# Four groups of PE signals moved from the last product to a drain, in two phases of a graph network kernel

## What is computed

```
x = layernorm(x + L0(x, edge_attr_64, src, dst, edge_type_32))   # relation attention
x = layernorm(x + L1(x, edge_index, 4))                          # four propagation steps
x = layernorm(x + L2(x, edge_index, edge_attr_128))              # gated convolution
x = layernorm(x + L3(x, edge_index))                             # two attention layers

# L0, its first part
h_proj = einsum('nd,rde->rne', h, relation_weight)
t_r = h_proj[etype, src]; h_r = h_proj[etype, dst]
# L2
z = concatenate([x[dst], x[src], edge_attr])
msg = sigmoid(z @ W_f + b_f) * softplus(z @ W_s + b_s)
out = relu(x + segment_sum(msg, dst))
```

## Time and profile before

| | us |
|---|---|
| median of 3 runs (7758.99 to 7787.47) | 7766.42 |
| span of the profiled execution | 7865.6 |
| PE busy in it | 4297.8 (55%) |
| DVE busy | 4772.7 (61%) |
| GpSimd busy | 3733.3 (47%) |
| ACT busy | 2362.7 (30%) |

### The profile page before, as it was taken

How to read it: one execution, slowest core, us unless ns; L and a number is a source line. 1 busy time by engine, 2 the same in 40 slices (tenths; PEclk the granted TensorE clock), 3 DMA queues, 4 the chain that set the end, 5 groups by cost and what they waited for, 6 DMA issues and landing times. The chain is left out here.

```text
span 7865.6 us, 104440 instructions
## 1 busy us (share of the span) xinstructions
PE 4297.8 (55%) x26852; PEld 3458.2 (44%) x26923; DVE 4772.7 (61%) x7334; ACT 2362.7 (30%) x3661; POOL 3733.3 (47%) x4217
## 2 busy tenths in 40 slices
PE   5777777310279545555535444444695444444397
PEld 2677776310179545555523222222683222222396
DVE  4666666688521156566547666666665766666675
ACT  5444444117322145555522111111222111111121
POOL 3666566100200166666625555553654555655363
PEclk9555555555589777777767666666896766666696
DMA  8677777895578533233225656564654666656462
GB/s 313 191 219 212 222 203 226 228 236 191 215 250 307 183 112 115 96 117 114 91 72 147 159 152 156 154 157 119 135 134 114 157 158 155 160 150 158 100 140 75
DMA packets 1472089, 1296.30 MB, mean 165 GB/s; under 512 B 1257993, under 2 KB 1297567, under 8 KB 1459038
## 3 DMA queue, kind: packets, MB, share of 16 engines
q1 hardware_dynamic: 902378, 671.59, 28.5%
q0 software_dynamic: 167008, 441.69, 21.0%
q10 hardware_dynamic: 402580, 181.62, 8.4%
HBM read 942.23 MB, written 351.27 MB: 164 GB/s over the span
## 5 line engine op out<-in xcount | busy, mean ns | idle before, releaser
L2503 POOL DMA_INDIRECT rows_p<-node_rows,stage_i x1632 | 1546.5, 948 | 1228.0 <-issue 978.9
L2557 PE MATMUL psZ<-parts_r,hot_t 128*128 x4896 | 1164.3, 402 | 1360.5 <-DVE lz L2638 867.7
L2557 PEld LDWEIGHTS psZ<-parts_r,hot_t 128*128 128x128 bf16 x4896 | 590.0, 121 | 1938.6 <-issue 1624.4
L2646 DVE TENSOR_TENSOR psZ<-psZ,rows_p 128x1320 f32<-128x1320 f32 x408 | 626.5, 1536 | 768.9 <-remote 283.0
L731 POOL DMA_INDIRECT rows_s<-hpx,hpST x784 | 741.4, 946 | 486.4 <-issue 203.8
L1961 POOL DMA_INDIRECT both<-table,srcI x784 | 741.9, 946 | 431.5 <-issue 211.1
L749 PE MATMUL psP<-window,pair_hot 128*128 x3136 | 701.9, 416 | 249.0 <-ACT pair_hot L771 146.6
L749 PEld LDWEIGHTS psP<-window,pair_hot 128*128 128x128 f32 x3136 | 672.8, 325 | 279.2 <-issue 279.0
L828 DVE SCALAR_TENSOR_TENSOR pair_run<-pair_run,same_c,psP 128x64 f32<-128x64 f32 x1568 | 440.2, 281 | 469.1 <-PE psP L749 209.1
L2953 PE MATMUL ps_steps<-A,xs 128*65 128x125 f32 x5184 | 578.8, 272 | 137.8 <-DVE A L2971 93.1
L2638 DVE SCALAR_TENSOR_TENSOR lz<-psZ,att 128x1320 f32<-128x1320 f32 (+2 forms) x428 | 642.6, 1501 | 8.4
(11 more groups left out here) (545 smaller groups left out, 7260.0 us busy)
## 6 DMA issues: line engine op xcount, KB each, us to landing
tile<-adj SPq DMA_DIRECT2D x168, 781.2 KB, 4.9
xs<-x_src SPq DMA_DIRECT2D x432, 128.0 KB
x_src<-rows_p SPq DMA_DIRECT2D x204, 256.0 KB
hpx<-stage ACTq DMA_DIRECT2D x25, 2048.0 KB
window<-hpx SPq DMA_DIRECT2D x196, 256.0 KB
dst_runs<-pair_run SPq DMA_DIRECT2D x28, 1792.0 KB
eaT<-in_ea SPq DMA_DIRECT2D x28, 1792.0 KB
adj<-tile SPq DMA_DIRECT2D x42, 781.2 KB
```

What stands on the lines that cost most here:

```text
L2503: pool.indirect_dma_start(rows[:, k, j, :], None, g.node_rows, bass.IndirectOffsetOnAxis(stage[:, k, j:j + 1], 0)).then_inc(got[k], 16)
L2557: last = pe.matmul(psZ[:, n % 2, j, 0:ZH], hot[:, k, col * CE:(col + 1) * CE], parts[:, bass.ds(at[col], 1), q, :].rearrange("p o c -> p ( ...
L2646: v.tensor_tensor(here, here, rows[:, slot, at * G:(at + 1) * G, 0:ZH], ALU.add).then_inc(added, 1)
```

## The change

The last product of four kinds of group no longer carries the increment. Behind it stands a drain of PE, an instruction of its own that ends once PE has finished all that was issued before it, and the drain carries the increment of the same semaphore by the same amount. In `Tiles.products` it is `counted`, in `relation_rows` `paired`, in `gated_convolution` `turned` and `made`. All waits, counts and other instructions stay.

```diff
@@ Tiles.products
             for e in range(2):
-                last = pe.matmul(self.bank(r, n)[:, j * TC:(j + 1) * TC], self.hot[:, k, st, :, e],
+                pe.matmul(self.bank(r, n)[:, j * TC:(j + 1) * TC], self.hot[:, k, st, :, e],
                                  self.hot[:, k, self.WIDE + st, 0:TC, e], start=e == 0, stop=e == 1)
-        last.then_inc(self.counted, 1)
+        pe.drain().then_inc(self.counted, 1)
@@ relation_rows, tensor
-                            last = pe.matmul(pair_sum(n, j), hot[:, n % 2, j * CE:(j + 1) * CE],
+                            pe.matmul(pair_sum(n, j), hot[:, n % 2, j * CE:(j + 1) * CE],
                                              window[:, n % 2, bass.ds(rel[j], 1), :].rearrange("p o c -> p (o c)"),
                                              start=True, stop=True)
-                        last.then_inc(paired, 1)
+                        pe.drain().then_inc(paired, 1)
@@ gated_convolution, tensor
-                                last = pe.transpose(psB[:, n % 2, j, :], both[:, k, m * G + j, :], g.ident[:, :])
-                            last.then_inc(turned, 1)
+                                pe.transpose(psB[:, n % 2, j, :], both[:, k, m * G + j, :], g.ident[:, :])
+                            pe.drain().then_inc(turned, 1)
...
-                                last = pe.matmul(psZ[:, q % 4, j, :], eaT[:, k, m * G + j, :], w2[:, :], start=False, stop=True,
+                                pe.matmul(psZ[:, q % 4, j, :], eaT[:, k, m * G + j, :], w2[:, :], start=False, stop=True,
                                                  skip_group_check=True)
-                            last.then_inc(made, 1)
+                            pe.drain().then_inc(made, 1)
```

## The result

The changed kernel takes **8064.16 us** (median of 4 runs, 8044.19 to 8074.15) against 7770.84 for the kernel before, measured beside it: ratio 1.036 [1.034, 1.038], or +293 us. The forecast was 7841 with a range to 8060. The sign was right; the size was four times too small.

The account below looks back on a forecast made before the run. It took GpSimd's gathers as the floor, with holes from held PE signals. Relation rows +205 and gated convolution -130 gave +75 us on the plain 7766: 7841 us, range 7660 to 8060 (the forecast's own 7730 to 7950).

Parts of the forecast that it names:

- relation rows become PE's series: Relation rows: PE's steps run serially behind drains, 7.3 us a batch instead of 6.26, +205 us over 196 batches.
- The load: Relation rows: register load of L741, no longer under products, adds 1.1 us a batch (0.65 to 1.65).
- a drain with the refill behind it: Relation rows: each drain taken at 0.2 us, refilling weights for each tile group at an estimated 0.1 us.
- the drain's bounds: One drain on PE costs 0.05 us (seen at a phase end) to 0.5 us (a whole L1735 product pair).
- not held: Gated convolution: drains' signals come promptly beside gathers, so a group takes 5.3 us instead of 5.95, -130 us.
- The sequencer's freedom: Where products' signals are held, PE's sequencer passes its own waits and loads; taken as evidence that drains escape.
- Rival 3: Drains held, PE standing with them: gated convolution +340 us, relation rows +450 atop +205, about 8760 us; chance 0.10.
- prompt psP: Relation rows: psP's signal comes promptly from its drain, worth nothing more there since PE bounds at 7.3 us.
- Rule against row: Skill's rule that matmul increments fire on completion, against signals 1.6 to 4.4 us late; if it held, 7971 us.
- rival 4: The hold exists only in the recording: no gains, serial PE costs +200 to +300, 8020 us; chance 0.05.

Follow-up runs that it names:

- f4: Kernel before with drains behind psB and psZ, gated convolution's gathers left out (half its input zero): 7593.45 us (one run) beside 7857.90.
- d2: Kernel before with only the drain behind psZ (`made`): 7882.01 us (one run), +109 us, beside 7773.38.
- e1: Kernel before with only the relation rows drains, behind psP and psA: 7182.61 us, ratio 1.0525, beside 6826.36.
- e2: Kernel before with only the gated convolution drains, behind psB and psZ: 6831.01 us, ratio 1.0009, beside 6826.36.
- e4: Kernel before with only the drain behind psZ (`made`): 6827.98 us, ratio 1.0002, beside 6826.36.
- d3: Kernel before with only the drain behind psB (`turned`): 7785.34 us (one run), +12 us, beside 7773.38.
- f3: Kernel before with only the next batch's register load issued earlier, behind the psP products, no drain added: 7859.05 us, ratio 1.0008.

## Why the prediction was right and wrong

**Right: relation rows become PE's series.** Forecast 7.3 us a batch and +205, measured (1582.3 - 201.1) / 196 = 7.05 and +154; the last tile product ended at 1582.3, against 1428.25. Two terms were too large. The load was taken at 1.1 us; it has a mean of 0.84 in the changed kernel and a median of 0.59. And a drain with the refill behind it was 0.3; the gaps show 0.21 to 0.26. (The kernel before has the load at a mean of 1.09 us, 79 of 196 over 1 us; in the changed kernel 49 are.) The low end of the drain's bounds, 0.05, fits what the drain itself does (0.02 us, and 0.10 to the next instruction). Where nothing is held, the same series costs +356, because the loop that it replaces is shorter there (5.02 us and not 6.25): the price of a serial engine is counted from the pace that it breaks, and that pace belonged to the session and not to the kernel.

**Wrong: "not held".** The step that failed is "I take 'not held', because what is held is the products' signal while PE's sequencer passes its own waits and loads". Forecast -130 us in gated convolution, measured +101: this term alone is 231 us off, more than the whole miss of 223. The rest nearly cancels: relation rows -51, the 38 us of neither phase, and 5 us between the medians of before. The sequencer's freedom was no evidence on a drain, since a drain asks for something that those waits and loads don't: the end of what PE has been given. f4 and d2 show it: drains of psZ outlast their products only with gathers beside them, and mostly end in GpSimd's rest (a median of 1.7 us after its last gather in d2).

**Rival 3, held and PE stands with it, is the mechanism**, at a third of its price. It had every psZ drain wait for the gathers' end and +340 us. 84 of 196 do. It depends on when the group ends. With a rest of GpSimd over 1 us taken as the end of a run, 82 of the 84 held drains of L2001 have their last product over 6 us after the run's start (median 7.5), and 90 of the 112 free ones between 3 and 6 us after it. The runs changed too: with a rest over 0.6 us as the end, 94 of 97 runs were of 8 gathers before, and 57 of 118 are of 4 now, so many groups finish in the free part. For relation rows rival 3 added +450 for holds; they came to 27 us, for the drains of psP end when GpSimd has already run out of work (it waits for them, 423.5 us) and those of the tiles early in a run. The forecast's prompt psP was right, but by luck: it rested on "not held", and what made it so is GpSimd's having stopped. In number the nearest forecast was rival 4's 8020, also by luck, since it has no loss in gated convolution.

**Rule against row.** "PSUM — Partial Sum Buffer", section "Engine vs sequencer instructions", of the Trainium skill has the increment on the matmul fire at completion and a drain wait for the idle engine. Where no gathers run, and in three sessions even where they do, both agree with the traces: a product's signal comes 13 to 14 ns behind it, a drain's the same behind the drain. Beside gathers in the other sessions the increments come 1.6 to 4.4 us behind the products' ends. Those ends are modelled, so the trace can't tell whether the rule's first half fails there or the products themselves complete late; that a drain is held too fits the second. The rule's second half is what makes a drain worse: what is late then is not only the signal but the instruction.

**Rival 4** (the hold is only in the recording) falls: the plain times differ between sessions by 945 us (7770.84 to 6825.51), and the stretches of gathers between the profile of before and those of e1, e2 and e4 by some 1000 us in all. Nor is the profiled execution the longer one: of the changed kernel it took 8044.19, the other three 8059.33 to 8074.15. What stays open: **why** a session holds. The kernel and its inputs are the same; in the holding sessions about half of the semaphore records are missing from the trace (63 to 68 thousand against 116 thousand), which goes together with the hold but needn't cause it. The third and fifth session name the same chip number with 6825.51 and 7857.90, so it may be a state and not a chip. Nor is it one level: the two attention phases' gathers last 1287 and 1295 us in d3 and 1303 and 1319 in f3, though neither edit touches them. No run here could choose it. The range was wrong by more than its edge: it left out rival 3, the mechanism that came, to which I gave 0.10.

## What to carry to other kernels

A drain is nearly free as an instruction (0.02 us behind the last product, 0.07 us for a second one); price it by what stands behind it on its engine, and above all by register loads, which cost 0.6 us and more once they are not under products. Put it only where the group behind it has slack against the engine that bounds the phase (behind psB it had, behind psZ not), or issue the next group's loads ahead of it. When a trace shows signals late for reasons that it doesn't name, don't assume that another carrier of the signal escapes them: measure one such instruction in that stretch first, and in more than one session.

## What the runs showed of the hardware

- One and the same kernel took 6820 to 6826 us in three sessions and 7771 to 7858 in three others; the difference that could be placed lies in stretches with back-to-back gathers of GpSimd.
- In the holding sessions a psZ drain beside gathers lasts up to 16.3 us, its own products included (2.1 at the median and 4.0 at most where no gathers run). The held ones end a median of 1.6 us after the last gather, and PE issues nothing meanwhile.
- Standing is not cost: 347 us at psB's drains left the phase as long as before (1156 against 1167 us), 467 us at psZ's made it 91 us longer; one profile each.
- The same edit is worth +0.0% or +1.4% (`made` alone, the latter one run), and +5.2% or +2.3% (relation rows), by the session. The whole change was only timed in holding sessions; the parts would give it some +5% in the others (356 + 5 us), which no run shows.
